# Turning the first two tiles of x on VectorE instead of TensorE

## The reference

```python
x = x + _L0_ffn_ref(_L0_cond_ref(x, itok_B_0_7, L0_cond_W, L0_cond_Wr, L0_cond_A, L0_cond_B), L0_ffn_route_w, L0_ffn_A, L0_ffn_Bw)
x = x + _L1_ffn_ref(_L1_cond_ref(x, itok_B_0_23, L1_cond_W, L1_cond_b, L1_cond_lora_As, L1_cond_lora_Bs), L1_ffn_W_base, L1_ffn_b_base, L1_ffn_W_router, L1_ffn_A, L1_ffn_B)
```

## Time and profile before

| | before |
|---|---|
| median of 3 runs | 484.27 us (483.86 to 485.82) |
| the profiled execution | 484.3 us |
| its span, first to last instruction | 482.1 us |
| TensorE / VectorE / ScalarE / GpSimd busy | 97% / 68% / 32% / 16% |
| granted TensorE clock, mean | 0.999 |
| DMA | 40.25 MB, mean 83 GB/s |

### The profile page before, as it was taken

The page is one execution under the profiler, slowest core; times in us unless marked ns, Lnnn a source line. Parts: engine busy times, 40 slices in busy tenths (PEclk is TensorE's granted clock), DMA queues, the critical chain, the costliest instruction groups (busy, mean ns, idle before and its releaser), DMA issues.

```text
span 482.1 us, 8344 instructions
## 1 busy us (share of the span) xinstructions
PE 465.5 (97%) x2911; PEld 430.1 (89%) x2911; DVE 327.2 (68%) x956; ACT 154.5 (32%) x340; POOL 75.5 (16%) x64
## 2 busy tenths in 40 slices
PE   6998999999999999999999999999999999999996
PEld 5987998999999789888999999999999999999985
DVE  3857755584776598849649848857865965963842
ACT  4565430232312364224223313323423323421320
POOL 2021000000000332221220240240221222130110
PEclk9999999999999999999999999999999999999999
DMA  8994548211112101223223321520520432300202
GB/s 268 384 286 163 143 142 148 105 44 45 44 45 52 42 16 28 31 44 111 46 46 107 50 46 61 95 44 16 133 43 7 122 46 33 110 2 2 103 2 87
DMA packets 88545, 40.25 MB, mean 83 GB/s; under 512 B 68503, under 2 KB 82465, under 8 KB 88382
## 3 DMA queue, kind: packets, MB, share of 16 engines
q1 hardware_dynamic: 88414, 39.81, 31.6%
q0 software_dynamic: 96, 0.00, 0.3%
HBM read 28.64 MB, written 11.16 MB: 83 GB/s over the span
## 4 chain that ended last, share of the span: by engine, by line
PE 77%; DVE 17%; issue 2%; ACT 2%; DMA 2%; SPq 0%; DVEq 0%; ACTq 0%
PE banks L1403 22%; PE banks L1405 22%; PE banks L1404 22%; PE banks L1419 4%; PE banks L1398 3%; DVE left L927 3%; DVE ybuf L1121 2%; DVE x_raw L978 2%; PE banks L1652 1%; PE banks L1455 1%; DVE b_acc L1218 1%; DVE G L927 1%; DMA fe_lo_dram<-fe_keep_lo 1%; DVE x_raw L1090 1%; ACT left L667 1%
## 5 line engine op out<-in xcount | busy, mean ns | idle before, releaser
L1403 PE MATMUL banks<-G,left 128*128 128x460 f32 x224 | 88.0, 393 | 0.0
L1404 PE MATMUL banks<-G,left 128*128 128x460 f32 x224 | 82.9, 370 | 0.0
L1405 PE MATMUL banks<-G,left 128*128 128x460 f32 x224 | 82.9, 370 | 0.0
L607 POOL TENSOR_TENSOR xTlo<-x_raw,xThi 128x512 fp32r<-128x512 f32 x28 | 41.1, 1486 | 252.3 <-ACT xThi L667 114.8
L1403 PE MATMUL banks<-WbThi,ws_hi 128*128 128x460 f32 (+1 forms) x216 | 75.2, 348 | 0.5 <-DVE Mdir L927 0.5
L1405 PE MATMUL banks<-WbThi,ws_lo 128*128 128x460 f32 (+1 forms) x216 | 73.4, 340 | 0.0
L1404 PE MATMUL banks<-WbTlo,ws_hi 128*128 128x460 f32 (+1 forms) x216 | 73.0, 338 | 0.0
L667 ACT ACTIVATE left<-x_raw 128x512 fp32r<-128x512 f32 x64 | 38.8, 628 | 64.1 <-DVE x_raw L1090 29.3
L1403 PEld LDWEIGHTS banks<-G,left 128*128 128x128 f32 x224 | 42.3, 189 | 4.5 <-DVE wzTlo L927 0.3
L1405 PEld LDWEIGHTS banks<-G,left 128*128 128x128 f32 x224 | 42.1, 188 | 4.6
L1404 PEld LDWEIGHTS banks<-G,left 128*128 128x128 f32 x224 | 42.3, 189 | 2.6
(11 more groups left out here) (213 smaller groups left out, 1004.6 us busy)
## 6 DMA issues: line engine op xcount, KB each, us to landing
x_raw<-in_x_dram SPq DMA_DIRECT2D x56, 128.0 KB, 3.6
out_dram<-ybuf SPq DMA_DIRECT2D x14, 512.0 KB, 2.8
x_raw<-in_L_cond_W_dram SPq DMA_DIRECT2D x10, 512.0 KB, 6.7
wraw<-in_L_cond_W_dram SPq DMA_DIRECT2D x5, 512.0 KB, 5.6
wraw<-in_L_ffn_W_base_dram SPq DMA_DIRECT2D x4, 512.0 KB, 10.2
x_raw<-in_L_ffn_W_base_dram SPq DMA_DIRECT2D x4, 512.0 KB, 9.3
a0f<-in_L_ffn_A_dram SPq DMA_DIRECT2D x2, 512.0 KB, 9.7
xin_first<-in_x_dram SPq DMA_DIRECT2D x1, 1024.0 KB, 15.3
```

Of the source, the lines that this page charges most:

```text
L607: return gp.tensor_tensor(out_, a, b, ALU.subtract)
L1403: pe.matmul(out_, l[0], r[0], start=start, stop=False, **kw)
L1404: pe.matmul(out_, l[0], r[1], start=False, stop=False, **kw)
L1405: return pe.matmul(out_, l[1], r[0], start=False, stop=stop, **kw)
```

## The change

The first two tiles are loaded in blocks of 32x32 by the helper that the other tiles use, with a semaphore for each tile. VectorE turns them in place in `xin_first`, and the high and low parts are made from there instead of from PSUM. TensorE's sixteen transposes of x are gone. Since `xin_first` now holds the turned x, x1 of the first batch is one addition for each quarter. The layout of x1 in `x1T_dram` becomes half by half, so that the two loads of it are of 4 KB a partition instead of eight pieces of 512 B. The parts of tile 1 are made early, beside tile 0's, and the Bw units move ahead of the small transpose of `wh`. In the diff below `xT_first_part` stands first for ScalarE (high parts), then for VectorE (low parts).

```diff
-            sp.dma_start(xin_first[:, :].rearrange("p (t d) -> p t d", t=2),
-                         xf[0:2 * P, :].rearrange("(t p) d -> p t d", p=P)).then_inc(x0_in, 16)
+            for half in range(2):
+                load_blocks(xin_first[:, half * D:(half + 1) * D], half, x01_in[half])
...
-                             x1T_dram.rearrange("p (k h c) -> p k h c", k=K, h=2)[:, :, half, :])\
+                             x1T_dram[:, half * D:(half + 1) * D].rearrange("p (k c) -> p k c", k=K))\
...
+            def xT_first_part(half):
+                for h in range(2):
+                    hi_half(x01_turned, half + 1, half_tiles(xT_first[0], half, h),
+                            raw_block(xin_first, half, h).rearrange("p (k c) -> p k c", k=4), xT_hi)
+
+            xT_first_part(0)
             for g in range(2):
                 if g == 0:
                     act.wait_ge(c0_done, 1)
...
+            xT_first_part(1)
...
-            xT_part(0, 0, xT_first, XT_FIRST[0])
...
-            xT_part(1, 1, xT_first, XT_FIRST[1])
-            whT_part(0, 0)
             copy_units(NEF + 10, units_bw)
+            whT_part(0, 0)
...
+            def xT_first_part(half):
+                for h in range(2):
+                    dve.wait_ge(xT_hi, half * 2 + h + 1)
+                    lo(half_tiles(xT_first[1], half, h), raw_block(xin_first, half, h).rearrange("p (k c) -> p k c", k=4),
+                       half_tiles(xT_first[0], half, h)).then_inc(xT_lo, 1)
+
+            for half in range(2):
+                dve.wait_ge(x01_in[half], 64)
+                turn_x(half, xin_first, x01_turned)
+            xT_first_part(0)
             dve.wait_ge(lang_in, 16)
...
-            xT_part(0, 0, xT_first, XT_FIRST[0])
+            xT_first_part(1)
...
-                dve.tensor_tensor(quarter(sums, g), bank, quarter(xT[1], g).bitcast(F32), ALU.add).then_inc(x1_half, 1)
-                dve.wait_ge(x1_half, g + 1)
-                dve.tensor_tensor(quarter(sums, g), quarter(sums, g), quarter(xT[0], g).bitcast(F32), ALU.add)\
-                   .then_inc(x1_sum, 1)
...
-                x1_first(g, X1W_FIRST[g], xT_first, xin_first)
+                x1_add(0, g, xin_first, X1W_FIRST[g])
...
             pe.wait_ge(c0_sum, 1)
-            pe.wait_ge(x0_in, 16)
-            turn_x(xin_first[:, 0:D], XT_FIRST[0])
...
-            pe.wait_ge(fe_lo, 1)
-            turn_x(xin_first[:, D:2 * D], XT_FIRST[1])
-            turn_small(wh_ready, 1, pt_wh, wh[:, :], twh_done)
             turn_units(NEF + 10, units_bw)
             fe_steps(10, 12)
+            turn_small(wh_ready, 1, pt_wh, wh[:, :], twh_done)
             small0(1, first_tiles(1))
...
-                        pe.wait_ge(x1_half, 1 + c)
+                        pe.wait_ge(x1_sum, 1 + c)
```

More of the change, by code:

```diff
@@ L179, in adaln_ffn @@
         wr0_in, a1_in, r1_in, bs_in = (sem(n) for n in ("wr0_in", "a1_in", "r1_in", "bs_in"))
-        x0_in = sem("x0_in")
+        x01_in = [sem(f"x{i}_in") for i in range(2)]
+        x01_turned = sem("x01_turned")
         w0_half_in = sem("w0_half_in")
@@ L199, in adaln_ffn @@
         as_hi, as_lo = sem("as_hi"), sem("as_lo")
-        tx_done, xT_hi, xT_lo = sem("tx_done"), sem("xT_hi"), sem("xT_lo")
+        xT_hi, xT_lo = sem("xT_hi"), sem("xT_lo")
         p0_done, h1_done = sem("p0_done"), sem("h1_done")
@@ L209, in adaln_ffn @@
         whT_hi, whT_lo = sem("whT_hi"), sem("whT_lo")
-        x1w_done, x1_half, x1_sum = sem("x1w_done"), sem("x1_half"), sem("x1_sum")
+        x1w_done, x1_sum = sem("x1w_done"), sem("x1_sum")
         x_turned = sem("x_turned")
@@ L791, in _ @@
             copy_units(NEF + 8, units_second[NEF - NU1 + 8:NEF - NU1 + 10])
[L792 removed]
+            copy_units(NEF + 10, units_bw)
             whT_part(0, 0)
[L794 removed]
             exp0(1)
@@ L957, in _, with turn_x @@
                     ins.then_inc(b0_lo, 1)
+            def turn_x(half, raw, turned=x_turned):
+                tile = raw[:, half * D:(half + 1) * D]
+                dve.transpose(tile, tile).then_inc(turned, 1)
+            def xT_first_part(half):
[7 more added lines that the diff above has]
+            xT_first_part(0)
             dve.wait_ge(lang_in, 16)
@@ L1077, in wzT_part, with x1_add @@
                 lo(wzTlo[:, :], pt_wz, wzThi[:, :]).then_inc(wzT_lo, 1)
-            def x1_first(g, bank, xT, sums):
-                dve.wait_ge(x1w_done, g + 1)
-                dve.tensor_tensor(quarter(sums, g), bank, quarter(xT[1], g).bitcast(F32), ALU.add).then_inc(x1_half, 1)
-                dve.wait_ge(x1_half, g + 1)
-                dve.tensor_tensor(quarter(sums, g), quarter(sums, g), quarter(xT[0], g).bitcast(F32), ALU.add)\
-                   .then_inc(x1_sum, 1)
-            def x1_add(q, g, raw):
+            def x1_add(q, g, raw, bank=x1w):
                 dve.wait_ge(x1w_done, q * 4 + g + 1)
-                dve.tensor_tensor(raw_quarter(raw, g), by_half(x1w), raw_quarter(raw, g), ALU.add).then_inc(x1_sum, 1)
+                dve.tensor_tensor(raw_quarter(raw, g), by_half(bank), raw_quarter(raw, g), ALU.add).then_inc(x1_sum, 1)
             def a_part(q, turn, nth, place=None):
@@ L1423, in _ @@
                 ins.then_inc(w0_used, 1)
-            def turn_x(src, at):
-                for h in range(2):
-                    for k in range(4):
-                        ins = pe.transpose(rows(at[h], k), rows(src, 4 * h + k), ident[:, :])
-                    ins.then_inc(tx_done, 1)
             pe.wait_ge(c0_sum, 1)
-            pe.wait_ge(x0_in, 16)
-            turn_x(xin_first[:, 0:D], XT_FIRST[0])
             pe.wait_ge(b0_lo, 1)
```

4 lines of the change are left out of this document (1 added, 3 removed).

## The result

| | before | after |
|---|---|---|
| median of the runs, us | 484.2 (483.86 to 485.82) | 493.27 (491.84 to 493.31) |
| profiled execution, us | 484.3 | 493.26 |
| its span, us | 482.1 | 491.4 |
| mean granted TensorE clock | 1.00 | 0.985 |

The changed kernel is slower by 1.8%: the ratio is 1.0184, interval 1.0167 to 1.0201. The forecast had the sign and the place, with 487.3 us and a range to 490.0; the time is 3.3 us above the range. The extra 9 us divide into three pieces, which the rows show one after the other.

What follows compares the result with a forecast made beforehand. TensorE, busy 97% of the span, was taken to bound the kernel, lengthened only where it must wait. 484.3 + 2.7 (first place) + 0.4 (late low parts) - 0.15 (second place) = 487.3 us, range 484.6 to 490.0.

Steps and rivals of the forecast that it cites:

- rival 2: TensorE's clock drops in the gap of about 4.25 us at the first sum: 2.5 us more, 489.8 us; chance 0.13.
- The first place: At the first sum ahead of D0, VectorE waits for tile 1 until 26.3 and D0 starts at 30.9: +2.7 us.
- the sentence on packets: At x's load, the skill page's packet overhead would land tile 1 at 24.2, run near 485.1; not used for the sum.
- Late low parts: Tile 1's low parts, made after the sums beside GpSimd's C0lo work, delay the first C0lo unit: +0.4 us.
- Second place: Eight transposes at 53.81 go, but the second Bw unit waits for VectorE's low part: only -0.15 of 0.87 us kept.
- x1 and the loads behind x: Four fewer VectorE x1 additions give nothing; loads queued behind x come later but are covered: nothing.
- The rival with the load hidden: Tile 1 of x lands before 23.9 us and the run is not slower, say 484.2 us; chance 0.17.
- The one with later loads late: SyncE held at the eight issues makes A1 or the B loads too late: about 2 us more, 489.3; chance 0.05.

Runs made afterwards that it cites:

- the kernels with runs of both kinds: Kernel before with three unused VectorE writes ahead of the first sum, 489.62 us; changed kernel with 34 unused 136-column TensorE products in the gap, 489.93 us.
- the filled run with 240 columns: Changed kernel with 32 unused TensorE products of 240 columns in the gap ahead of the sums: 487.57 us.
- the new order: Changed kernel with VectorE's sums ahead of tile 0's low parts, tile 1 turned behind them, its parts made near 40 us: 483.70 us.
- the four with fills: Changed kernel with unused TensorE products in the gap, of 136 (two placements), 272 or 240 columns: 489.93, 487.69, 487.92, 487.57 us.
- the last run: Changed kernel with VectorE's sums first and, on top, whTlo made ahead of the fe_lo store's wait and memset: 482.10 us.

## Why the prediction was wrong

**The step that failed is rival 2.** Its mechanism was stated rightly and left out of the sum, with a chance of 0.13 and a price of 2.5 us. With that price in the sum the forecast would have been 489.8 us, still 3.5 too low.

The chance: the clock fell in every run of the changed kernel, in every run with a wait of 2.4 us or more, in all four with 1.8 us (plain loads) and in five of nine with 2.2 us. A gap forecast at 4.25 us lay well past that. The kernel before had a row that bears on it, which neither the forecast nor its rows show. The longest wait of TensorE behind its start is this one, and the clock stays at 1.00 behind it:

```profile
43.80 0.66 PE L1398 MATMUL banks<-ident,x_raw 128*128 128x128 f32 x4 [1.26 <-DVE ws_lo L927]
```

```profile
44.00:46.00 2.00, 2.00 (x20) 1.00 0.00 0
```

(A stretch: TensorE's busy us and count, clock, DMA share, GB/s.) So the trace had a wait of 1.26 us with the clock up behind it and nothing at all on 4.25 us; 0.13 had nothing under it.

The price: it was the loss of the fold's first products at the start. Behind the gap the clock stayed at 0.50 for 13 us, although TensorE was nearly always busy, and the kernels with runs of both kinds put that at 5.1 and 5.4 us. The start itself was slow for longer than the forecast counted. TensorE's first instructions there are three pairs of transposes from 4.33 to 7.76, 3.43 us; the like three pairs at the high clock take from 30.70 to 32.80, 2.10 us:

```profile
4.33 0.88 PE L1398 MATMUL banks<-ident,a0f 128*128 128x128 f32 x3 [4.33 <-DMA routers<-in_L_ffn_route_w_dram]
...
7.76 0.59 PE L1419 MATMUL banks<-R0T,ws_hi 128*128 128x272 f32 x1
...
30.70 0.51 PE L1398 MATMUL banks<-ident,a0c 128*128 128x128 f32 x3
```

With them the slow start is 9 us long and lost some 3.7 us (1.3 + 24 x 0.1), an estimate from these rows, where the forecast had 2.5. The sentence that the profile's granted clock can't tell was too broad: it reads 1.00 at the start, where the products are slow, but it shows the fall behind a gap in each trace here that has one.

**The first place.** The order of events was as forecast: turn, low parts, cast and bias, sum, D0. The shift at D0 is +3.3 against +2.7 in the forecast's terms, since the second tile landed at 27.1, not 26.3. The eight loads ran at the rate that was taken: b0raw landed at 19.7 (6.59 + 13.1), the fourth load of x at 23.6 and the eighth at 27.1, so eight took 7.4 us, 0.93 us each against the forecast's 0.94. What was mis-sized is the start of the count, 18.8. The rows of SyncE's queue for it, with b0raw's time to landing:

```profile
6.59 0.47 SPq L409 DMA_DIRECT2D b0raw<-in_L_cond_B_dram  x1
DMA to landing us min/median/max: 13.1/13.1/13.1
7.10 16.80 SPq L405 DMA_DIRECT2D xin_first<-in_x_dram  x8
```

b0raw landed 0.9 us later than in the kernel before, though it is still issued ahead of x. The first load of x, issued 0.5 us behind it, landed at 20.3, 0.6 us behind it; that the two hold each other up is likely and not shown.

The forecast also gave the change the whole 1.09 us of the transposes ahead of D0. By the timeline D0 came 0.85 us behind their start (27.13 to 27.98), so with a free load the first place loses 0.5 us and not 0.25. The run with the plain loads bears that out: D0 starts at 28.40 there, +0.4.

On the sentence on packets: the estimate from the Trainium skill ("DMA: Bandwidth & Descriptors", "Measured"; its figure is for transfers issued from GpSimd) had the second tile landing at 24.2; it came 3 us later. The choice of the trace's rate over the page's was right.

**Late low parts, +0.4.** Both were slowed beside GpSimd, as feared, but not alike: 0.79 and 1.83 us against 0.63. In the changed kernel their cost can't be told from the low clock. In the filled run with 240 columns TensorE takes 6.55 us from D0 to small0 (32.10 to 38.65) against 6.40 (27.98 to 34.38), and 7.95 us to the small0 product of the next unit against 7.52, with new waits of 0.4 us for C0lo and 0.4 us for WbTlo. But the new order has the same two waits and 6.59 and 7.99 us, and the kernel before with the transposes moved has them too, and in neither do low parts of the second tile stand there. So the 0.4 us are real and the cause that I gave them is not: the three share that TensorE doesn't turn the first tile ahead of D0. Those transposes seem to have given the units behind them time that they now wait for.

**Second place, -0.15.** Nothing came of it (3.24 us against 3.21). The wait that took the place of the transposes is 0.91 us, as long as they were.

**x1 and the loads behind x, nothing.** Right, each by a run of its own (493.16 with the additions doubled, 484.13 with the loads alone).

**Not in the sum: the store of fe_lo, +0.8.** VectorE's wait for it is 4.99 to 5.01 us in the changed kernel and in those of its kin without fills (one tile behind, plain loads, x1 twice, new order), 3.8 to 4.2 in the kernel before and its kin, 3.1 in the four with fills, and 4.3 in the last, where VectorE comes to it later. The store moves the same 580 KB each time. That it reached the end by whTlo is borne out by the last run, where TensorE's wait of 1.2 us is gone and the time falls by 1.6; why the store takes longer stays open.

**Without the clock** the forecast of 487.3 looks better than it was. Runs of the changed kernel with the gap filled and the clock up took 486.9 to 489.2 us, but 1.2 us of that closeness is luck: in those kernels TensorE doesn't wait for whTlo. The terms as measured, timeline against timeline, give 484.3 + 3.6 + 0.4 + 0.8 = 489.1 us, of which the last is the store that the forecast left out.

The rival with the load hidden (0.17) is ruled out by the landing at 27.1. The one with later loads late (0.05) is ruled out too, though its mechanism was there: SyncE was held for 16.8 us at the eight issues, and A1 was issued at 26.37 instead of 15.93. But it landed at 36.2, 4.3 us later than before, and its first use is at 45.96.

## What to carry to other kernels

Price a change that moves work off TensorE not by what it saves there, but by the wait that it leaves at the next place where TensorE needs another engine: here 1.96 us were taken off and a wait of 4.8 us was made, because a turn, two low parts and a bias stood ahead of the one sum that mattered. Put what TensorE waits for first in the queue of its engine, and what nobody waits for behind it; the new order alone took 9.6 us back, about half of it the clock's. And where a change makes TensorE stand still for longer than any wait after which the trace shows the full clock, count the lowered clock in the sum and not as a rival, with its price for the stretch that follows: here waits of up to 1.26 us left it up, and from 1.8 us on it fell in 29 runs of 33.

## What the runs showed of the hardware

- The granted clock fell to 0.50 in all runs behind stand-stills of 2.4 to 6.9 us and of 1.8 us (four runs), in five of nine at 2.2 us, and in none behind 1.26 us or 0.9 us. Length alone does not settle it: with narrow products in the gap it fell in two runs of four behind a stand-still of 0.7 us. It can fall a microsecond or two after TensorE is busy again (second tile turned behind the sums: busy from 29.3, fall near 31.7).
- It came back only after 6 to 15 us of nearly always busy TensorE, with products of 136 columns and transposes. At the start of the same kernel TensorE is slow for 9 us (4.33 to about 13.3), and the profile's granted clock reads 1.00 there.
- The low stretch cost 5.1 and 5.4 us, each from runs of both kinds of one kernel.
- The Trainium skill ("TensorE: Matmul & The Clock Gate", "What's actually happening") says of the rise at a start that the transition depends on where in a free-running count the work lands, and so varies from run to run. For the fall, the nine runs of one kernel, four at one level and five at the other, fit that and don't prove it.
- Eight block loads of 128 KB in pieces of 128 B landed 0.93 us apart, 141 GB/s, and held SyncE for 16.8 us at their issues; the plain load of 1 MB held it for 5.71 us.
- A wait of VectorE for one and the same store of 580 KB was 3.1, 3.8 to 4.2 or 5.0 us in the traces, alike within each group of kernels; no cause was found.
